# A two-way WKV scan with a binarized product: the order of GpSimd's last steps, and who adds up the last rows

## The reference

```python
tf    = sigmoid(sum(time_emb))                      # one number per batch
decay = exp(-exp(w)) * (0.5 + 0.5 * tf)             # per batch and channel
ek, ekv = exp(min(k, 30)), exp(min(k, 30)) * v
# a forward and a backward scan over time for each of the two: a = a * decay + ekv
euk = exp(min(u + k, 30))
num = nf + nb - ekv + euk * v
den = df + db - ek + euk
base = sigmoid(r) * num / max(den, 1e-8) * (0.8 + 0.2 * tf)
bw   = where(weight >= 0, 1, -1) * mean(|weight|, row)
out  = x + base @ bw.T + bias
```

## Time and profile before

| what | value |
| --- | --- |
| device time, median of 3 runs | 540.99 us (540.88 to 542.02) |
| device time of the profiled execution | 542.2 us |
| its span | 540.1 us |
| VectorE busy | 505.4 us, 94% of the span |
| ScalarE, GpSimd, TensorE busy | 391.5, 385.0, 366.2 us |
| DMA | 92.65 MB, mean 172 GB/s |

### The profile page before, as it was taken

The page is one execution under the profiler, slowest core; times in us unless marked ns, Lnnn a source line. Parts: engine busy times, 40 slices in busy tenths (PEclk is TensorE's granted clock), DMA queues, the critical chain, the costliest instruction groups (busy, mean ns, idle before and its releaser), DMA issues.

```text
span 540.1 us, 5413 instructions
## 1 busy us (share of the span) xinstructions
PE 366.2 (68%) x1797; PEld 212.0 (39%) x1803; DVE 505.4 (94%) x384; ACT 391.5 (72%) x433; POOL 385.0 (71%) x209
## 2 busy tenths in 40 slices
PE   2323333224778979777777979857689988899950
PEld 2222222123444435444344544534455545344420
DVE  5999999999999999999999999999999999998923
ACT  2869798897859999999779697968658755855000
POOL 0157776667758777887777788777878887981846
PEclk9999955555688797879897998988789998999985
DMA  7655477665466888899988798797879898992995
GB/s 214 176 156 142 137 190 191 163 168 130 99 145 137 179 186 176 181 194 194 187 167 167 144 192 179 176 190 175 181 116 226 188 239 166 180 171 40 165 282 175
DMA packets 125923, 92.65 MB, mean 172 GB/s; under 512 B 2860, under 2 KB 117576, under 8 KB 125896
## 3 DMA queue, kind: packets, MB, share of 16 engines
q0 software_dynamic: 30720, 33.56, 39.5%
q1 hardware_dynamic: 89976, 56.12, 35.7%
q10 hardware_dynamic: 5200, 2.62, 1.8%
HBM read 58.74 MB, written 16.78 MB: 140 GB/s over the span
## 4 chain that ended last, share of the span: by engine, by line
DVE 64%; issue 19%; PE 6%; DMA 5%; POOL 2%; ACT 2%; POOLq 0%; DVEq 0%; SPq 0%; ACTq 0%
DVE pair L809 24%; DVE pair L823 13%; DVE pair L835 7%; DVE wkv L852 6%; DVE own L836 6%; DVE pair L832 5%; DMA k_nat<-in_L_ffn_bias_dram 4%; DVE euk L858 2%; PE prod L455 1%; PE kT L455 1%; PE prod L412 1%; DVE y_start L815 1%; POOL acts L375 1%; ACT rec L631 1%; PE kT L387 1%
## 5 line engine op out<-in xcount | busy, mean ns | idle before, releaser
L412 PE MATMUL prod<-acts,sgn 128*128 128x512 f16 x768 | 195.6, 413 | 7.1 <-POOL acts L308 3.2
L823 DVE TENSOR_TENSOR_SCAN pair<-cols,y_start,pair 128x1024 f32<-128x1024 f32 x64 | 150.1, 2346 | 1.3 <-DVE y_start L815 0.2
L809 DVE TENSOR_TENSOR_SCAN pair<-cols,pair 128x1024 f32<-128x1024 f32 x64 | 142.8, 2272 | 0.0
L412 PEld LDWEIGHTS prod<-acts,sgn 128*128 128x128 f16 (+1 forms) x768 | 80.8, 106 | 103.8 <-issue 28.1
L338 POOL TENSOR_TENSOR wkv<-euk,rec 128x1024 f32<-128x1024 f32 x31 | 77.3, 2493 | 32.6 <-ACT rec L633 32.6
L348 POOL TENSOR_TENSOR wkv<-wkv,rec 128x1024 f32<-128x1024 f32 x31 | 73.2, 2362 | 38.2 <-ACT wkv L672 38.2
L387 PE MATMUL kT<-ident,k_nat 128*128 128x128 f32 x256 | 47.4, 346 | 74.4 <-DVE own L836 74.4
L359 POOL TENSOR_TENSOR wkv<-wkv,pair 128x1024 f32<-128x1024 f32 x31 | 73.4, 2369 | 18.7 <-DVE wkv L852 18.5
L308 POOL TENSOR_TENSOR acts<-wkv,rec 128x1024 f16<-128x1024 f32 x30 | 75.1, 2505 | 0.0
L631 ACT ACTIVATE rec<-euk,lnb 128x1024 f32<-128x1024 f32 x31 | 35.6, 1149 | 51.3 <-DVE euk L858 38.6
L387 PEld LDWEIGHTS kT<-ident,k_nat 128*128 128x128 f32 x256 | 38.6, 180 | 82.2 <-issue 81.6
(11 more groups left out here) (107 smaller groups left out, 554.9 us busy)
## 6 DMA issues: line engine op xcount, KB each, us to landing
pair<-own POOLq DMA_DIRECT2D x32, 512.0 KB, 4.6
k_nat<-in_fside_BxSxS_dram SPq DMA_DIRECT2D x30, 512.0 KB, 4.4
x_nat<-in_x_dram SPq DMA_DIRECT2D x29, 512.0 KB, 5.9
o_nat<-in_x_dram POOLq DMA_DIRECT2D x24, 512.0 KB, 6.3
out_dram<-o_nat SPq DMA_DIRECT2D x21, 512.0 KB, 5.2
x_end<-in_x_dram SPq DMA_DIRECT2D x9, 512.0 KB, 6.2
y_fm<-in_L_ffn_weight_dram SPq DMA_DIRECT2D x8, 512.0 KB, 6.5
x_nat<-in_L_ffn_bias_dram POOLq DMA_DIRECT2D x3, 512.0 KB, 7.0
```

The costliest lines, as they stand in the source:

```text
L412: ins = pe.matmul(prod[:, h, :], view[:, c, m % CT * P:m % CT * P + P], acts[:, part, m // CT % 2 * CT + c, h * H:(h + 1) * H], start=(par ...
L809: dve.tensor_tensor_scan(buf, d, buf, 0.0, ALU.mult, ALU.add).then_inc(st["F" + kind], 1)
L823: dve.tensor_tensor_scan(buf[:, ::-1], d, buf[:, ::-1], y_start[:, i:i + 1], ALU.mult, ALU.add)\
```

## The change

Four things are changed:

1. In steps 26 to 29 low_half stands in front of base (the flag "late" is gone), as in most other steps.
2. The bias DMAs have a table, TAILS: block q is done in step 25 + q for q = 0 to 5, block 6 in step 30 beside block 5, block 7 in step 31. None is left for the time after the last step. x_tail(7) moves from k_nat1 to the fourth slot of x_end, free once s_turn(29) has read it, and SP loads x_tail(6) in step 29, x_tail(7) in step 30.
3. For v = 8 to 11 VectorE adds park to the bank itself (a new operation, L932 of the changed kernel), before the multiplication by orow. GpSimd keeps v = 12 to 15.
4. At the start of the last phase ScalarE's halves of tile 30 are cut in two (prior_halves), the second one late; VectorE's prior_lo(1) moves behind v = 0; TensorE does across(6) after the first three ended blocks and not before them, and ended(3) and ended(4) before across(7).

```diff
+    TAILS = {25: (0,), 26: (1,), 27: (2,), 28: (3,), 29: (4,), 30: (5, 6), 31: (7,)}
...
-            a = x_nat[(j + 2) % NX] if j < 3 else k_nat[j - TT + 2]
+            if j == TT - 1:
+                return x_end[:, 3, :]
+            a = x_nat[(j + 2) % NX] if j < 3 else k_nat[0]
...
-                if n >= N - 2:
-
-                    done(sp, "kT", n)
-                    load_tail(TT - N + n)
+                if n == N - 3:
+
+                    done(sp, "kT", N - 2)
+                    load_tail(TT - 2)
+                if n == N - 2:
+
+                    done(sp, "sT", N - 3)
+                    load_tail(TT - 1)
...
-                if n >= N - TT + 2:
-                    biases(n - N + TT - 2)
+                for j in TAILS.get(n, ()):
+                    biases(j)
...
-                if low and not first and not late:
+                if low and not first:
                     low_half(n - 2, p)
...
-                if late:
-                    low_half(n - 2, p)
...
-            for j in range(TT - 2, TT):
-                biases(j)
             pool.wait_ge(st["orow_sb"], 1)
-            for i in range(CT):
+            pool.wait_ge(st["early_sb"], CT)
+            for i in range(CT // 2, CT):
...
+            def prior_halves(i):
+
+                t = time_half(i)
+                high = acts[:, 0, (N - 2) % (2 * CT), t]
+                done(act, "base", N - 2)
+                act.mul(high, wkv[0][:, t], 1.0 / LO_GAIN).then_inc(st["prior_hi"], 1)
+                act.wait_ge(st["prior_hi"], i + 1)
+                act.mul(rec[0][:, t], high, LO_GAIN).then_inc(st["prior_hib"], 1)
...
             last_inverse(0)
-            done(act, "base", N - 2)
-            halves(N - 2, 0)
+            prior_halves(0)
             last_inverse(1)
             last_halves(0)
+            prior_halves(1)
             last_halves(1)
...
-            prior_lo(1)
...
+                if TT <= v < TT + CT // 2:
+                    dve.wait_ge(st["early_sb"], CT)
+                    dve.tensor_tensor(bank[v % TT], bank[v % TT], park[v - TT], ALU.add).then_inc(st["whole"], 1)
+                    dve.wait_ge(st["whole"], v - TT + 1)
...
-                if v >= TT:
-                    dve.wait_ge(st["joined"], v - TT + 1)
+                if v >= TT + CT // 2:
+                    dve.wait_ge(st["joined"], v - TT - CT // 2 + 1)
...
                 if v == 0:
+                    prior_lo(1)
                     last_lo(1)
```

More of the change, by code:

```diff
@@ L167, in bi_wkv_binary_ffn @@
             "ln", "rec", "chk", "two", "inv", "gate", "base", "hi", "hib", "lo",
-            "prod", "ev", "yT", "yc", "abs", "sgn", "wT", "wTc", "orow", "orow_sb", "early", "early_sb", "soon", "nat", "weighed", "joined",
-            "scaled", "res", "prior_lo", "last_den", "last_ln", "last_rec", "last_chk", "last_inv", "last_gate", "last_base",
+            "prod", "ev", "yT", "yc", "abs", "sgn", "wT", "wTc", "orow", "orow_sb", "early", "early_sb", "soon", "nat", "weighed", "whole", "joined",
+            "scaled", "res", "prior_hi", "prior_hib", "prior_lo", "last_den", "last_ln", "last_rec", "last_chk", "last_inv", "last_gate", "last_base",
             "last_hi", "last_hib", "last_lo")}
@@ L338, in step @@
                     pool.tensor_tensor(W, euk[1 - p][:, :], R, ALU.mult).then_inc(st["chk"], 1)
-                if n >= N - TT + 2:
-                    biases(n - N + TT - 2)
+                for j in TAILS.get(n, ()):
+                    biases(j)
                 first = n % CT == 1
-                late = N - 6 <= n < N - 2
                 if low and first:
@@ L367, in _ @@
                 residuals(summed(n))
-            for j in range(TT - 2, TT):
-                biases(j)
             pool.wait_ge(st["orow_sb"], 1)
-            for i in range(CT):
+            pool.wait_ge(st["early_sb"], CT)
+            for i in range(CT // 2, CT):
                 j, h = TT // 2 + i // 2, i % 2
                 o = slice(h * H, (h + 1) * H)
-                pool.wait_ge(st["early_sb"], i + 1)
                 pool.tensor_tensor(park[i], park[i], orow[:, o], ALU.mult).then_inc(st["weighed"], 1)
-                pool.wait_ge(st["weighed"], i + 1)
+                pool.wait_ge(st["weighed"], i - CT // 2 + 1)
                 pool.wait_ge(b_in[j], 16)
@@ L559, in _ @@
             across(5, bank[5], range(CT - 2), True, False)
-            pe.wait_ge(st["last_gate"], 1)
-            across(6, bank[6], range(CT - 2), True, False)
             def ended(v, lo):
                 across(v, bank[v % TT], range(lo, CT), v >= TT, True).then_inc(st["nat"], 1)
+            pe.wait_ge(st["last_gate"], 1)
             pe.wait_ge(st["prior_lo"], 1)
@@ L570, in _ @@
                 ended(v, CT - 2)
+            across(6, bank[6], range(CT - 2), True, False)
+            for v in range(3, 5):
+                ended(v, CT - 2)
             pe.wait_ge(st["last_gate"], 2)
             across(7, bank[7], range(CT - 2), True, False)
-            for v in range(3, TT):
+            for v in range(5, TT):
                 ended(v, CT - 2)
@@ L892, in prior_lo @@
                 t = time_half(i)
-                done(dve, "hib", N - 2)
+                dve.wait_ge(st["prior_hib"], i + 1)
                 dve.tensor_tensor(acts[:, 1, (N - 2) % (2 * CT), t], wkv[0][:, t], rec[0][:, t], ALU.subtract)\
```

## The result

The changed kernel takes 525.2 us (median of 4, 524.99 to 526.39), the kernel before beside it 540.93 (4 runs, 540.34 to 542.02): the ratio is 0.9711, with 95% from 0.969 to 0.9733. It is 15.7 us faster; 17.6 was forecast, and the time is 1.8 us above the forecast 523.4. The profiled execution took 526.39 us with a span of 524.6, against 540.1 before: 15.5 us.

The account below looks back on a forecast made before the run. VectorE, busy 94%, was taken as the bound up to about 498 us, then the bias DMA and GpSimd's joins. Steps 5.0 plus last phase 12.6 gave 17.6 us off 540.99: 523.4, range 519.5 to 529.5.

Parts of the forecast that it names:

- The clamps: Steps 27 to 30: each VectorE clamp falls from 2.85 to 0.74 us, at most 8.4 us in all.
- the 0.3 for two gaps of VectorE: Steps 28 to 30: two VectorE gaps of about 0.25 us beside the clamps, counted as 0.3 us gained.
- Step 25: A bias DMA issue in front of low_half and inv delays the gate: VectorE loses 0.5 us.
- The first clamp's 2.1 us goes into a longer gate wait: Step 27: VectorE's gate waits for a late inv, expected 2 to 2.5 us, so the shorter clamp gains 0.
- The den term: Step 27: den is held until GpSimd's base ends, 1.1 us lost; bounds 0.2 and 1.2.
- the bound of 0.2: Step 27: lower bound for den's loss beside base, reading the row at 360.67 as a mild slowing.
- Nothing in the change makes kT of tile 27 earlier: Step 27: TensorE's kT, set by its units waiting for ScalarE at 397.14, stays as late as before.
- I take 527.5: End of span in the old clock, from VectorE's chain 526.4 and DMA sum 527.3; last phase gains 12.6 us.
- B: Rival: DMA engines are the bound; 2 us lost in the steps, 3 in the end: 528.4 us; chance 0.25.
- A: Rival: step 27's lateness is caught up, den not held; steps give 8.1 instead of 5.0: 520.3 us; chance 0.17.
- C: Rival: a bias DMA waits for its load in front of inv, holding gate and VectorE: 541 to 545; chance 0.02.
- D: Rival: the end stays with a late third x DMA add instead of the bias: 536 to 541; chance 0.03.

Follow-up runs that it names:

- e5: Changed kernel with step 25's bias DMA of block 0 issued behind inv instead of in front of low_half: 525.35 us.
- e3: Changed kernel with part 3 undone, so GpSimd joins all eight pieces and VectorE adds none: 526.06 us.
- e11: The changed kernel run again, unaltered, on another set's chip: median 525.31 us.
- e2: Kernel before with part 2 alone (bias DMA table, the two loads, x_tail(7) moved): 533.43 us.
- e4: Changed kernel with the three x-adding DMAs issued right behind the last base, not behind last_lo; joins stay: 522.76 us.
- e10: Changed kernel with early x adds, GpSimd joining all eight, and bias 0 behind inv in step 25: 521.36 us.
- e12: Repeat of the changed kernel with early x adds and GpSimd joining all eight: 521.90 us.
- e7: Changed kernel with low_half behind base again in step 27 alone: 526.78 us.
- e6: Changed kernel with part 4 undone (ScalarE's halves in one piece, prior_lo(1) and across(6) where they were): 525.55 us.
- e8: Changed kernel with x adds issued early and part 3 undone, so GpSimd joins all eight pieces: 521.72 us.

## Why the prediction was right in the main, and 1.8 us off

**The clamps.** Right: 4 x 2.1 us, all at 0.74. Steps 28 to 30 gained 6.32 us, where 6.3 + 0.3 stood in the sum; the 0.3 for two gaps of VectorE did not come. Nor did the 0.2 on den of step 30, which the sum had left out (1.32 us now, 1.34 before).

**Step 25.** Right: 0.5 us forecast, 0.55 measured, shown to be the bias DMA's by e5.

**Step 27.** "The first clamp's 2.1 us goes into a longer gate wait" was half wrong. The den term was right (0.96, 1.1 taken), so the bound of 0.2, a mild slowing, is out; and the Trainium skill's rule on who interferes with whom (SBUF — State Buffer, "Who interferes with whom"), which gave 1.1 to 1.2, was the better guide than the nearest row. The row at 360.67 did not speak against it: den met base for 0.38 us there (base ended at 361.05) and took 0.22 longer, here it met it for 1.11 us and took 0.96 longer. The bound of 0.2 had carried the price of a short meeting over to a long one.

But the gate waited 0.71 us, not 2.4, and the step gave 0.68 where -1.1 was forecast. What failed is the step from "Nothing in the change makes kT of tile 27 earlier" to a fixed start of kT. Nothing in the change did, but the clock does: kT began 4.24 us ahead of the clamp of step 27, not 2.58, and the 1.66 us are the difference of the two gate waits. The 2.4 was worked out from one execution of before, in which TensorE's clock had fallen behind its 2.34 us wait; the trace of before showed this (turns of 1.91 us), and I read it as fixed. e1, with part 1 alone, has the short wait, and e3 and e11, the latter the very kernel that was forecast, have the long one with 2.38 and 2.37 (in e11 kT begins 2.57 us ahead of the clamp, 404.01 and 406.58). So both cases belong to the kernel, and the forecast had one of them as certain. It was a size taken from one draw, worth 1.66 us. The steps came to 6.46 instead of 5.0.

Which case comes goes with the length of TensorE's wait for ScalarE in step 26: in the runs where it was 0.61 to 1.78 us (eleven executions: the changed kernel's first, e1, e2, e4 to e10 and e12) the turns behind it took 1.04 us, and where it was 1.95, 1.98 or 2.34 they took 1.91 to 1.92. In e3 and e11 as in before, the granted clock from 396 to 404 us is 0.79. Why the wait's length differs between executions of one kernel is open; the products just ahead of it ran at different paces too (3.62 us for sixteen in e11, 4.49 in the changed kernel's first profile), which only moves the question to an earlier stretch.

**The last phase.** VectorE's start of v = 0 was right: 491.23 in the changed kernel's clock is 497.29 in that of before (474.11 - 468.05 = 6.06 to be added), 497.3 forecast. Its end is 524.9 in that clock, 523.9 forecast, 1.0 late. The new addition took 0.69 to 0.72 with its gap (0.7 taken), GpSimd's joins were covered, and there was no wait of GpSimd for own DMAs or loads. The chain's 1.0 us is spread over it: a block takes 1.37 us on average, not 1.34, and the wait at v = 5 is 1.30.

The mis-sized term is the end, "I take 527.5". It was 524.6 + 6.06 = 530.7. Two estimates stood side by side, VectorE's chain at 526.4 and the DMA sum at 527.3, and only the second was the bound. What was low in that sum is the price of an adding DMA, the rate, and the tail. The three adds took 12.8 us of engine time, 4.3 each, where 3.6 each had been taken from the rows of before; the stores took a little less than forecast (11.6 and 5.4, not 12.0 and 5.8). That is 29.9 us of work (shares of 40 us in the queue rows), not 28.6: 1.1 us at the forecast rate. The first packet moved at 496.1, 502.2 in the clock of before, not 502.0: 0.2. The last store landed at 523.9, so the 29.9 us took 27.8, or 1.08 per us, not 1.13: 1.4. And the last store's landing is not the end of the span, 0.7 us follow. Together 3.4 us, which is 530.7 less the sum's 527.3, and 3.2 more than the 527.5 taken. Why an add cost more here and the rate was lower is open. By the sign that the prediction set ("or the last o_nat store lands over 3 us after VectorE's last store, it is B"): the last rows' store was issued at 518.9, the o_nat store landed 5.0 us later. Counted from that store's landing (523.4) it is 0.5 us only, and in e7, whose last phase is the same code, SP waits 1.2 us for the rows' store after the o_nat store has landed. So it is all the late transfers together, and not the one store, that hold the end. In this sense the last phase was of rival B's kind, in the end and not in the steps, where nothing piled up.

That it is these DMAs is shown by e4, which moves only the issue of the x adds: 2.4 us less, and the end 2.5 us behind VectorE. Its VectorE runs as in the changed kernel, so the 2.4 us lay between VectorE's end and the span's. That e4's last phase gives the 12.6 us of the forecast is chance: there VectorE's chain is the bound, which had been forecast at 526.4 and came 1.0 late, near the 527.5 that had been taken for another reason.

The forecast's two errors had opposite signs: 1.5 us too little from the steps, 3.2 too much from the end. 5.0 + 12.6 became 6.46 + 9.44, of which 0.4 went to a later start of step 25: 15.5 for 17.6. That the time came within 1.8 us of the forecast is in part luck. With the long gate wait that was forecast, the profiled execution of e11 took 527.61 us, 3.0 above the 524.6 that were forecast for a profiled one; the changed kernel's first, with the short wait, took 526.39.

**The rivals.** A (the steps give 8.1) was half there: no long gate wait, but den held. B would have cost 2 us in the steps and 3 in the end: about 3 came in the end, none in the steps. C, a wait of a bias DMA for its load, did not come up. D was right that the third x add is a late one (it landed at 516.3), but its store landed at 523.9, 530.0 in the clock of before, and not at 535 to 540; even before, with the two bias DMAs in the queue, it had landed at 533.3.

**Parts 3 and 4.** The prediction's sum put them in VectorE's chain, and did not say what they are worth. e3 and e6 say: little here, as the chain isn't the end (0.9 us, partly the other clock case, and 0.35, neither clear of the spread), and part 4 doesn't end it earlier. Once it is, part 3 is a loss of 1.0 us (e8 against e4). Part 4 was not tried there.

## What to carry to other kernels

Where two estimates of an end lie within a microsecond, work out the worse one as carefully as the better, with the landing of the last transfer in it; and if the late transfers depend on nothing that is late, issue them before the burst (2.4 us here for one moved wait). An adding DMA whose result must still be stored is two transfers in a row and belongs ahead of stores that end with themselves. A wait read from one execution, behind which the clock had fallen, is one of two cases: carry both into the range. And before work of GpSimd is moved into a gap, see what VectorE does in that gap: a meeting with an operation that reads two tensors from SBUF cost VectorE about 1 us each here, one with the clamp 2.1.
